# A GpSimd subtraction in a segmented-memory attention layer that waits for one more VectorE result

## What is computed

```python
qs, ks, vs, qnope, knope = map(to_segs, (rope(q), rope(k), v, q, k))
def step(carry, inp):
    mem, z = carry
    q_s, k_s, v_s, qn_s, kn_s = inp
    scores = where(mask, einsum('bhnd,bhmd->bhnm', q_s, k_s) * SCALE, -inf)
    sdpa = softmax(scores) @ v_s
    sq = elu(qn_s) + 1
    mem_out = (sq @ mem) / (sq @ z + 1e-6)
    out = beta * mem_out + (1 - beta) * sdpa
    sk = elu(kn_s) + 1
    prev_v = (sk @ mem) / (sk @ z)
    mem = mem + sk.T @ (v_s - prev_v)
    z = z + sk.sum(axis=2)
    return (mem, z), out
```

## Time and profile before

| | us |
|---|---|
| median of 3 runs | 2598.22 (2596.3 to 2605.95) |
| the profiled execution, its own time | 2596.41 |
| its span, first to last instruction | 2594.6 |
| the 128 steps of the memory layer, seen on PE | 1756 to 2410 |

### The profile page before, as it was taken

One profiled execution on the slowest core, in us unless ns is written; L12 is line 12 of the kernel. 1 busy time (PEld: TensorE's weight loads), 2 busy tenths in 40 slices (PEclk: granted clock), 3 DMA queues, 4 the chain that ended last, 5 costly groups with the idle time before them and its releaser, 6 DMA issues. The chain is left out here.

```text
span 2594.6 us, 70531 instructions
## 1 busy us (share of the span) xinstructions
PE 2171.0 (84%) x26096; PEld 1526.0 (59%) x26096; DVE 1671.3 (64%) x5435; ACT 1433.3 (55%) x3704; POOL 1190.4 (46%) x1203
## 2 busy tenths in 40 slices
PE   6589958589973899999899987948999999999696
PEld 3288844368972233434343335936777777878396
DVE  6722247643226787888788834357889998898522
ACT  5455544265544255555455554536777777777353
POOL 2156654136655030120100002648888888888264
PEclk8699978779996699999999987979999999999798
DMA  4011120001125211111120001123333333333113
GB/s 134 33 40 44 43 87 4 33 27 43 44 60 174 82 44 38 44 39 38 32 51 20 20 1 51 43 82 89 110 108 106 107 109 102 110 106 105 45 41 93
DMA packets 95831, 167.43 MB, mean 65 GB/s; under 512 B 21193, under 2 KB 36232, under 8 KB 93064
## 3 DMA queue, kind: packets, MB, share of 16 engines
q1 hardware_dynamic: 81920, 135.10, 18.2%
q0 software_dynamic: 13568, 27.81, 3.7%
q10 hardware_dynamic: 8, 0.00, 0.0%
HBM read 65.19 MB, written 32.79 MB: 38 GB/s over the span
## 5 line engine op out<-in xcount | busy, mean ns | idle before, releaser
L1544 ACT ACTIVATE ca_pt<-ca_ps 128x512 f32<-128x512 f32 (+3 forms) x768 | 341.3, 491 | 319.6 <-PE ca_ps L1649 136.6
L734 PE MATMUL ffn_ps<-ffn_xst,ffn_up_w 128*128 128x128 f32 x3392 | 421.6, 278 | 0.4 <-issue 0.4
L734 PEld LDWEIGHTS ffn_ps<-ffn_xst,ffn_up_w 128*128 128x128 f32 x3392 | 403.4, 195 | 1.8 <-issue 1.7
L857 DVE TENSOR_TENSOR ffn_hid<-ffn_sg,ffn_ps 128x512 f32<-128x512 f32 x212 | 145.8, 688 | 366.9 <-PE ffn_ps L742 107.8
L576 POOL DMA_INDIRECT ffn_xs<-ffn_x,ffn_token_at x212 | 205.9, 971 | 308.6 <-DVE ffn_token_at L840 165.9
L581 POOL DMA_INDIRECT ffn_y<-ffn_ys,ffn_result_at x212 | 209.4, 988 | 129.3 <-DVE ffn_ys L863 69.3
L643 ACT ACTIVATE ffn_sg<-ffn_ps 128x512 f32<-128x512 f32 x212 | 125.8, 594 | 245.8 <-remote 205.8
L1645 PE MATMUL ca_ps<-ca_stacks 75*128 75x512 bf16 (+3 forms) x768 | 245.0, 342 | 17.6 <-ACT ca_pt L1544 10.1
L1777 DVE TENSOR_REDUCE ca_m_far<-ca_ps 128x1 f32<-128x128 f32 (+5 forms) x384 | 236.6, 616 | 30.6 <-PE ca_ps L1623 28.2
L1623 PE MATMUL ca_ps<-ca_stacks 72*128 72x512 bf16 (+3 forms) x768 | 223.5, 356 | 33.5 <-DVE ca_m_near L1778 21.1
L1778 DVE CUSTOM_DVE_ANT_0 ca_spill<-ca_ps,ca_bias_q 128x256 f32<-128x256 f32 (+1 forms) x512 | 201.1, 398 | 9.7 <-PE ca_ps L1623 9.7
(11 more groups left out here) (343 smaller groups left out, 4771.3 us busy)
## 6 DMA issues: line engine op xcount, KB each, us to landing
im_mates<-im_t SPq DMA_DIRECT2D x256, 128.0 KB, 2.1
im_mem_by<-im_mem SPq DMA_DIRECT2D x248, 130.0 KB
ffn_got<-ffn_y SPq DMA_DIRECT2D x48, 256.0 KB, 5.8
ca_stacks<-scratch_q_piece SPq DMA_DIRECT2D x16, 576.0 KB
ca_stacks<-scratch_k_piece SPq DMA_DIRECT2D x48, 192.0 KB
ffn_x<-ffn_xn SPq DMA_DIRECT2D x32, 256.0 KB, 2.0
w_w<-in_L_ffn_experts_w_dram SPq DMA_DIRECT2D x2, 2048.0 KB, 11.4
ffn_xs<-ffn_x,ffn_token_at POOLq DMA_INDIRECT x212
```

The source lines that it names most:

```text
L734: last = nc.tensor.matmul(ps[:, bank, j * P:j * P + P], up_w[:, n % WS, first + j * P:first + j * P + P], xst[:, n % 2, :], start=True, st ...
L1544: nc.scalar.activation(pt[:, i % 8, lo - c0:hi - c0], ps[:, tile_bank(i), lo - c0:hi - c0], ACT.Exp, scale=SCALE).then_inc(p_ready, 1)
```

## The change

GpSimd's surprise(j) waits for one more semaphore, `pn_ready`, which DVE's scale_p(j) raises when it has written the normalised softmax weights. surprise doesn't read those weights. Nothing else is changed: no work is added or removed, and every queue keeps its order.

```diff
                 def surprise(j):
 
+                    pool.wait_ge(S["pn_ready"], j + 1)
                     pool.wait_ge(S["known"], j + 1)
                     pool.wait_ge(S["lifted"], j + 1)
                     new = uu[:, j % 2, :, 0:D]
```

## The result

The change makes the kernel faster: 2579.41 us in the median of 5 runs (2573.44 to 2582.95) against 2598.22 of 5 runs before (2589.79 to 2605.95). The ratio is 0.9929, 95% interval 0.9901 to 0.9958, which is 11 to 26 us. Measured once more beside the experiments it is 0.9943, interval 0.9911 to 0.9976. The profiled execution took 2582.95, 13.5 less than that of before.

The account below looks back on a forecast made before the run. PE was taken as the main limit, with the two-iteration loop through m1 0.62 us longer in iterations with an add. Gains 9.9 + 1.0 + 2.8 + 0.8 + 0.2 = 14.7 took 2598.22 to 2583.5, range 2576 to 2592.

Parts of the forecast that it names:

- The mechanism: surprise on Pool and scale_p on DVE hinder each other; the second to start pays; unhindered, scale_p takes 0.29.
- The middle stretch: 96 iterations with one product each: 22 groups of four gain 0.45 each, 9.9 us, plus an estimated 1.0 for the rest.
- Before the products: Iterations ahead of the first product: a pair falls from 9.79 to 9.39, seven pairs gain 2.8 us.
- Two products each: Iterations with two products, 43.23 us: PE is busy throughout, so gain 0.
- The last stretch: The last 19.65 us: two pairs gain 0.8 and the last steps 0.2.
- the fourth rival: rotate's waits for late mates, 7.4 us, all come through to PE: gain only 7.3, 2591; chance 0.08.
- Pool's cost: Later surprise on Pool: iteration 4.87, least 4.65, under PE's 4.94 and the 4.70 before the products, so cost 0.
- The hand-over: From scale_p's end on DVE to surprise's start on Pool: 0.08, as for spread.
- the rival that made it dear, and slower: Waking Pool after scale_p costs more: from 0.52 the kernel is slower, at 0.8 it takes 2630; chance 0.04.
- The rule: DVE with two SBUF inputs and GpSimd reading SBUF exclude each other; scale_p would end 0.29 after surprise, but ended 0.15 after.
- the second rival: Before the products features holds scale_p to 1.56, Pool needs 4.79; gain 1.5 instead of 2.8, 2584.8; chance 0.06.
- PE alone is left: Middle stretch falls to 474.2, a gain of 18.0 there and 21.8 in all, 2576.4; chance 0.08.

Follow-up runs that it names:

- order only: Kernel before, with surprise waiting for the reciprocal of the softmax sums, so it starts just behind scale_p's start and runs beside it; ratio 0.9948.
- a wait already met: Kernel before, with surprise waiting for a semaphore raised an iteration earlier, a wait that never holds; ratio 1.001.
- no surprise: Kernel before, with surprise's subtraction cut to one element, order and waits unchanged; ratio 0.994.
- the second profile: The changed kernel run and profiled once more beside the experiments; ratio to the kernel before 0.9943, layer 630.44 us.
- wait but at adds: Kernel before, with the new wait in all steps but those in which DVE also adds an output block; ratio 0.9954.
- statistics last: The changed kernel, with the row statistics moved behind recall on DVE; ratio to the kernel before 0.9891.
- wait at adds: Kernel before, with the new wait only in iterations in which DVE also adds an output block (28 of the 124); ratio 0.9949.
- wait for the transpose: Kernel before, with surprise waiting for the transpose behind scale_p, so later than with the change; ratio 0.9955.

## Why the prediction was right, point by point

- **The total.** Forecast 2583.5, measured 2579.41, inside 2576 to 2592. The forecast gain of 14.7 is to be held against the layer, 13.0 (two profiles of the change 0.3 apart), and against 0.9943, 14.8. Of the 1.7 that the layer lacks 1.25 are the last stretch and 0.5 the middle. The 18.8 between the medians is wider than what the layer shows; its interval reaches down to 11.
- **The mechanism** was right: who starts second pays (*order only*), it isn't the further wait as such (*a wait already met*), and nothing else of surprise costs time (*no surprise*).
- **The middle stretch.** The add's iteration was to keep 0.17 and the group to take 19.86; it takes 19.86, and the 22 x 0.45 stand as a sum: of the 17 regular groups the nine clean ones gain 0.43 in the mean, the five with an add and statistics in one iteration 0.3, and the three with statistics elsewhere 0.7. The add's own iteration keeps 0.19 over 4.93, and the next one makes up 0.05 of it. With 1.0 for the rest it was 10.9; measured 10.4 and, again, 9.9. The rest was a guess, and what became of it differs from profile to profile.
- **Before the products.** 9.39 was forecast for the pair, 9.40 measured; 2.8 for the stretch, 2.65 and 3.67 measured. That 2.65 lies so near is luck. The run-up pairs, which the sum left out, gain too: the second profile, *order only*, *no surprise*, *wait but at adds* and *statistics last* take 84.91 to 85.05, a gain of 3.5 to 3.7. In the first profile PE stands still for 0.73 in iteration 6, for nothing that the profile shows:

```profile
1780.07 0.41 PE L2134 MATMUL im_ps<-g_ident,im_m 128*128 128x128 f32 x2 [0.73 <-issue]
```

- **Two products each:** 0 forecast, 0.2 measured.
- **The last stretch** is the step that failed: a gain of 1.0 forecast, a loss of 0.25 measured, of 0.49 in the second profile. It failed twice over. First, 0.40 were taken for each of two pairs and 0.2 for the last steps. But steps 124 to 127 have no surprise, and there the kernel before has an unhindered scale_p already:

```profile
2396.60 0.69 DVE L2276 TENSOR_TENSOR im_pn<-im_pe_,im_rs 128x128 f32<-128x128 f32 x1
2401.58 0.29 DVE L2276 TENSOR_TENSOR im_pn<-im_pe_,im_rs 128x128 f32<-128x128 f32 x1
```

  The second pair of before takes 9.66 and the first 10.05; with no late transfer both take 9.65, so that only the first gains. Second, the sum put late transfers at nothing. In the changed kernel's profile rotate waits there 0.98 for its mates, and Pool then takes part of it into the next iteration:

```profile
2379.34 1.27 POOL L2028 TENSOR_TENSOR im_rope_qk<-im_t,im_mates 128x512 f32<-128x512 f32 x1 [0.98 <-DMA im_mates<-im_t]
2380.57 1.26 POOL L2034 TENSOR_TENSOR im_el<-im_ee,im_rr 128x512 f32<-128x512 f32 x1
2382.07 0.68 POOL L2021 TENSOR_TENSOR im_uu<-im_uu,im_lift 128x256 f32<-128x256 f32 x1 [0.23 <-DVE im_pn L2277]
```

```profile
2380.64 0.69 DVE L2269 TENSOR_TENSOR im_t<-im_ps,im_cs 128x512 f32<-128x512 f32 x1 [0.85 <-POOL im_rope_qk L2028]
2381.45 0.54 DVE L2277 TENSOR_TENSOR im_pn<-im_pe_,im_rs 128x128 f32<-128x128 f32 x1
```

  cosines waits 0.85 for rotate, scale_p runs into features, and that iteration of PE takes 5.70 where its neighbours take 4.61. In the second profile of the change rotate waits 1.22 at the same place. That is the mechanism of the fourth rival, *late transfers*. Where no transfer was late there, *order only*, *no surprise* and *wait but at adds* took 19.23 to 19.27, so 0.4 of the 1.0 is there to be had (0.7 with the statistics moved). Why the transfer is late stays open.
- **Late transfers in the middle stretch.** rotate waited 4.0 us for mates, less than the 7.4 of before, so at its full price that rival is refuted. Its mechanism isn't. The five waits of up to 0.58 cost nothing. The two long ones, 1.20 in iteration 29 and 1.32 in 69, came through: Pool's features is late, PE waits for it before lift_keys, and iterations 30 and 70 take 5.39 and 5.68 instead of 4.93.

```profile
2094.80 1.27 POOL L2028 TENSOR_TENSOR im_rope_qk<-im_t,im_mates 128x512 f32<-128x512 f32 x1 [1.32 <-DMA im_mates<-im_t]
2096.03 1.27 POOL L2034 TENSOR_TENSOR im_el<-im_ee,im_rr 128x512 f32<-128x512 f32 x1
```

```profile
2097.35 0.44 PE L2205 MATMUL im_ps<-g_ident,im_el 128*128 128x128 f32 x2 [0.52 <-POOL im_el L2034]
```

  That is 1.2 us of the middle stretch, and 0.3 more in iteration 62, ahead of which rotate stood 1.01 and the profile names PE's score as what ended it. The kernel before had a wait of 1.04 in iteration 69 too, and lost nothing by it (its iteration 70 takes 5.14; 5.17 and 5.18 are usual for an iteration with the same statistics); only its longest, 1.63 in iteration 80, cost some 0.6. Where the difference comes from can be read in part: rotate(69) starts 0.30 behind PE's score(68) before and 0.85 with the change; of these 0.55, 0.25 are that DVE's sines starts later against PE, which stands still less, and 0.30 that the mates land later behind it. The prediction named PE waiting at lift_keys as a sign that Pool's iteration is the longest; it shows, in three of 96 iterations. *Order only* and *no surprise* lose 0.6 to 0.8 in iteration 70 as well, *wait at adds* and *wait but at adds* 0.4; the second profile of the change has no such wait there and takes 4.93.
- **Pool's cost.** Its iteration was to be 4.87 behind ACT and 4.65 at least, both under PE's pace. Before the products Pool's iterations alternate between 4.61 and 4.78, and *wait for the transpose* showed the same sum at its limit, 4.95 for 4.99 reckoned. As a rule Pool cost 0, as forecast; behind a long wait for mates it did not. learn's wait for surprise doesn't appear among the waits of the middle stretch.
- **The hand-over** is 0.08, as taken from spread; the rival that made it dear, and slower, is refuted.
- **The rule.** Measured, a scale_p that starts 0.88 behind features' start ends 1.42 after it (*wait for the transpose*), as was reckoned from the row, and not at 1.56 as full exclusion would have it; the second rival, and the price worked out beside the rule of the Trainium skill (SBUF — State Buffer, Who interferes with whom), is refuted. In *order only* surprise ends at 2052.05, where fully blocked it would end 0.68 after scale_p's end, at 2052.18. The trace agrees with the page that the one issued first goes through unhindered and the other pays, and both times finds some 0.13 less than the full block.
- **PE alone is left** (18.0 in the middle) is refuted: 481.83 against 474.2. What is left are the 0.13 of each add, the statistics (0.25 more, five times), the late transfers (1.2 to 1.5) and irregular groups.

## What to carry to other kernels

Where a short instruction on one of DVE and Pool stands in the loop that closes and a longer one of the other engine has slack (here both read two SBUF tensors; no other kind was run), look at which of the two starts first: a wait that only turns the order can give back the whole hindrance, if the delayed one's slack (here 0.57 behind the transpose) is larger than the delay. Price such a gain not by the busy time it frees (31.6 us here) but by the iterations in which the loop through that instruction is longer than the limit: a quarter of the waits brought all that the clean groups gained. And look at what the gain eats into: with the limiting engine's stalls gone, a late transfer that the loop had swallowed can come through (a wait of 1.04 cost nothing before, those of 1.20 and 1.32 cost 0.5 and 0.8 with the change; part of that is that the transfers were later).

## What the runs showed that was not expected

- **The rest of the kernel varies more than the change.** Span less layer is 1950.9 us in the profile before and 1950.4 in that after, but 1935.9 to 1938.9 in the eight profiles of the experiments, with nothing changed there. Most of that lies ahead of the layer: its first score starts at 1757.99 in the first profile of the change and at 1748.21 in the second. The medians of before in the two sets of experiments, 2586.56 and 2589.12, are lower too. The cause stays open.
- **Some groups are irregular, at the same iterations in most kernels.** Of the groups from iterations 28, 32, 80 and 84 at least two lie up to 3 us above clean ones in each kernel (21.47, 20.66, 22.53, 20.56 before; 20.33, 20.40, 21.06, 20.72 with the change; in its second profile 20.07, 20.65, 22.66, 20.58). In most of them PE stands still, within a run of equal matmuls or between two runs, for nothing that the profile shows, in the second profile of the change so:

```profile
PEld im_ps L2150 <- issue: 2.3, 2, 1.4
...
PE im_ps L2150 <- issue: 1.7, 2, 1.1
```

  The group from 28 in both profiles of the change is long mainly by its late transfer (waits of 1.20 and 0.93 in iteration 29), and so is the group from 68 in the first (20.55; 19.86 in the second). Standstills and late transfers together make sums over the 96 iterations uncertain by 1 to 3 us; largely by them the sums of five experiments lie 0.3 to 2.2 above their ranges.
